# One Trainium2 core, a Mamba block and a graph-gated mixture of experts: the last stage scales the experts' outputs by their gates on ScalarE and VectorE, and the gates are made in another order

## The reference, cut to what matters

```
agg    = segment_sum(h[src] * alpha, dst) + b_gat            # alpha: softmax of the edges that end in dst
scores = layernorm(agg, ln_gamma, ln_beta).reshape(M, HEADS, NUM_EXPERTS).mean(1)
topk_s, topk_i = top_k(scores, 2);  w = softmax(topk_s)
for ei in range(4):
    g   = where(topk_i == ei, w, 0).sum(-1)
    out = out + g * (gelu(x @ W1[ei] + b1[ei]) @ W2[ei] + b2[ei])
```

## Time and profile before

| | |
|---|---|
| time, median of 3 runs | 4289.58 us (4286.68 to 4291.24) |
| the profiled execution: its own time, its span | 4290.37 us, 4288.4 us |
| PE, DVE, ACT busy over the span | 68%, 71%, 36% |
| TensorE's mean granted clock | 0.819 of full |
| the last block in the span | 4094.94 to 4288.4 us |
| of it: sums landed, then gates | 4101.67 to 4163.76 us |
| of it: mixing to the last `ost` | 4163.76 to 4285.95 us |

### The profile page before, as it was taken

How to read it: one execution, slowest core, us unless ns; L and a number is a source line. 1 busy time by engine, 2 the same in 40 slices (tenths; PEclk the granted TensorE clock), 3 DMA queues, 4 the chain that set the end, 5 groups by cost and what they waited for, 6 DMA issues and landing times. The chain is left out here.

```text
span 4288.4 us, 30277 instructions
## 1 busy us (share of the span) xinstructions
PE 2896.4 (68%) x9220; PEld 1468.0 (34%) x9220; DVE 3026.0 (71%) x4723; ACT 1552.8 (36%) x2238; POOL 1345.1 (31%) x1414
## 2 busy tenths in 40 slices
PE   6988798999999899897648155445545544453019
PEld 2433343444444344343335022223322322232019
DVE  8899879887888697978664556546645654664565
ACT  2332145444445444444454033223223322322117
POOL 0000000000000000001111677777777777777600
PEclk9998899999999999998768567767767776776559
DMA  5113123445454455466546321122112111111237
GB/s 177 69 69 115 57 89 95 145 147 171 145 176 146 155 158 191 155 183 236 191 148 221 28 44 37 37 45 47 37 37 54 37 37 45 27 18 18 23 140 285
DMA packets 341083, 454.19 MB, mean 106 GB/s; under 512 B 82749, under 2 KB 256712, under 8 KB 332090
## 3 DMA queue, kind: packets, MB, share of 16 engines
q1 hardware_dynamic: 289290, 389.20, 28.2%
q0 software_dynamic: 51632, 63.07, 7.8%
HBM read 340.70 MB, written 111.42 MB: 105 GB/s over the span
## 5 line engine op out<-in xcount | busy, mean ns | idle before, releaser
L1487 POOL DMA_INDIRECT got<-scratch_tab,src_at x1280 | 1223.6, 956 | 390.0 <-issue 378.4
L691 PE MATMUL in_ps<-tokens,w_in 128*128 128x512 f32 x2048 | 938.4, 610 | 20.3 <-ACT zst L898 15.6
L1441 PE MATMUL hid_ps<-tokens,w 128*128 128x512 f32 x512 | 314.1, 746 | 834.9 <-ACT hid L1669 812.2
L618 POOL MEMSET tokens<- 1x128 int32 x1 | 0.2, 194 | 1899.9 <-DVE tokens L1073 1899.9
L691 PEld LDWEIGHTS in_ps<-tokens,w_in 128*128 128x128 f32 x2048 | 394.4, 197 | 501.9 <-issue 501.9
L708 PE MATMUL out_ps<-w_out,act 128*128 128x512 f32 x1024 | 476.9, 609 | 4.6 <-DMA w_out<-in_m_WoutT 4.5
L1072 DVE TENSOR_TENSOR tokens<-tokens 128x1024 f32<-128x1024 f32 x380 | 464.4, 1222 | 9.7 <-ACT tokens L856 8.7
L1073 DVE TENSOR_TENSOR tokens<-tokens 128x1024 f32<-128x1024 f32 x380 | 464.0, 1221 | 0.0
L1441 PEld LDWEIGHTS hid_ps<-tokens,w 128*128 128x128 f32 x512 | 107.7, 234 | 928.7 <-ACT hid L1669 822.1
L1594 DVE TENSOR_TENSOR hold<-by_value,is_loop 128x256 f32<-128x256 f32 x20 | 8.5, 425 | 581.7 <-ACT by_value L1680 581.7
L1680 ACT ACTIVATE by_value<-got 128x1536 f32<-128x1536 f32 x20 | 80.5, 4027 | 743.6 <-DMA got<-scratch_tab,src_at 743.6
(11 more groups left out here) (270 smaller groups left out, 4053.6 us busy)
## 6 DMA issues: line engine op xcount, KB each, us to landing
w_out<-in_m_WoutT SPq DMA_DIRECT2D x256, 512.0 KB, 4.7
w_in<-in_m_WinT SPq DMA_DIRECT2D x128, 512.0 KB, 4.0
scratch_y<-ys SPq DMA_DIRECT2D x25, 1024.0 KB, 4.0
got<-scratch_tab,src_at POOLq DMA_INDIRECT x1280
tokens<-scratch_xt SPq DMA_DIRECT2D x8, 2048.0 KB, 9.4
scratch_sz<-zst SPq DMA_DIRECT2D x64, 256.0 KB, 5.4
gz<-scratch_sz SPq DMA_DIRECT2D x64, 256.0 KB, 5.1
tokens<-scratch_y SPq DMA_DIRECT2D x16, 1024.0 KB, 8.6
```

Of the source, the lines that this page charges most:

```text
L691: last = t_.matmul(in_ps[:, z, :], w_in[:, n % WIN, k, :], xT[:, s % 2, k, :], start=(k == 0), stop=(k == KC - 1))
L1441: last = t.matmul(hid_ps[:, f], w1[:, e, f * P:(f + 1) * P], tokens[:, g * QW:(g + 1) * QW], start=True, stop=True)
L1487: g.indirect_dma_start(got[:, y, t, :], None, tab_d[:, :], bass.IndirectOffsetOnAxis(ap=src_at[:, y, t:t + 1], axis=0))\
```

## The change

Mixing: ScalarE scales the outputs of expert 0 by its gate (`first2`) and those of expert 2 (`third`); VectorE multiplies expert 1 by its gate and adds that into `first2` (L1944), and multiplies expert 3 for a whole block at once (`fourth`, L1932, called `fourths(q)` below). TensorE adds three products with the plain identity as the moving operand, which turns and adds. `first2` and `third` hold eight chunks, `ost` now four blocks, `fourth` two; they lie in the memory of tiles that the gates have done with. Gates: the parameters' wait stands ahead of the one for the sums, with three tiny operations behind it; ScalarE squares while VectorE multiplies by gamma; the mean over heads is two folds ahead of the scaling by the root; the ranking works on three, two and one pairs of neighbours at once; some links merge.

One wait per four products has become two per three. SP issues the same transfers in the same order. The diff:

```diff
...
-            ost = sb("ost", [P, 2, QW], F32, st)
-            diag = sb("diag", [P, 4, EXP, P], F32, st)
...
+            by_gamma = found_f[:, 0:BINS * H16].rearrange("p (n x) -> p n x", x=H16)
+            pairs = agg_f.rearrange("p n x -> p (n x)")[:, 0:BINS * H16 // 2].rearrange("p (n x) -> p n x", x=H16 // 2)
+            agg_c = agg_f.rearrange("p n x -> p (n x)").rearrange("p (x c d) -> p x c d", x=2, d=P)
+            first2, third = agg_c[:, 0], agg_c[:, 1]
+            ost = found_f[:, 0:4 * QW].rearrange("p (x n) -> p x n", n=QW)
+            fourth = found_f[:, 4 * QW:6 * QW].rearrange("p (x n) -> p x n", n=QW)
...
-                    sp.dma_start(out[b][:, h * QW:(h + 1) * QW], ost[:, q % 2, :]).then_inc(s_out[q % 2], 16)
+                    sp.dma_start(out[b][:, h * QW:(h + 1) * QW], ost[:, q % 4, :]).then_inc(s_out[q % 4], 16)
...
-                        t.wait_ge(s_ring[q % R], 16 * (q // R + (1 if q % R >= SLOTS else 0)))
                     if q >= 2:
                         t.wait_ge(s_fin, q - 1)
+                    t.wait_ge(s_four, q + 1)
                     for c in range(CH):
                         n = CH * q + c
+                        to = out_ps[:, q % 2, c * P:(c + 1) * P]
+                        t.matmul(to, fourth[:, q % 2, c * P:(c + 1) * P], ident[:], start=True, stop=False)
+                        t.wait_ge(s_da, n + 1)
+                        t.matmul(to, third[:, n % 8], ident[:], start=False, stop=False)
                         t.wait_ge(s_dv, n + 1)
-                        t.wait_ge(s_da, n + 1)
-                        for e in range(EXP):
-                            last = t.matmul(out_ps[:, q % 2, c * P:(c + 1) * P],
-                                            rings[q % R][:, e * QW + c * P:e * QW + (c + 1) * P],
-                                            diag[:, n % 4, e, :], start=(e == 0), stop=(e == EXP - 1))
-                        last.then_inc(s_mix, 1)
+                        t.matmul(to, first2[:, n % 8], ident[:], start=False, stop=True).then_inc(s_mix, 1)
...
+                s.wait_ge(s_cent, 1)
+                s.activation(agg2, agg_f, ACT.Square).then_inc(s_cent, 1)
...
+                    y = rings[q % R].rearrange("p (e n) -> p e n", e=EXP)
+                    if q >= SLOTS:
+                        s.wait_ge(s_ring[q % R], 16 * (q // R + (1 if q % R >= SLOTS else 0)))
                     for c in range(CH):
                         n = CH * q + c
-                        if n >= 4:
-                            s.wait_ge(s_mix, n - 3)
-                        for e in range(EXP // 2, EXP):
-                            j = CH * order[q] + c
-                            op = s.activation(diag[:, n % 4, e, :], ident[:], ACT.Copy, scale=g_tok[:, e, j:j + 1])
-                        op.then_inc(s_da, 1)
+                        j = CH * order[q] + c
+                        if n >= 8:
+                            s.wait_ge(s_mix, n - 7)
+                        s.activation(first2[:, n % 8], y[:, 0, c * P:(c + 1) * P], ACT.Copy, scale=g_tok[:, 0, j:j + 1])\
+                            .then_inc(s_first2, 1)
+                        s.activation(third[:, n % 8], y[:, 2, c * P:(c + 1) * P], ACT.Copy, scale=g_tok[:, 2, j:j + 1])\
+                            .then_inc(s_da, 1)
...
+                v.wait_ge(s_nw, 48)
+                ck(v.tensor_reduce(shift[:], params[:, 2, :].rearrange("p (h e) -> p e h", e=EXP), AX.X, ALU.add))
+                v.tensor_scalar(shift[:], shift[:], 1.0 / HEADS, None, ALU.mult)
+                ck(v.tensor_scalar(params[:, 1, :], params[:, 1, :], 1.0 / HEADS, None, ALU.mult))
...
-                for h in range(HEADS):
-                    op = v.tensor_tensor(agg[:, :, h, :], total[:, :, h, 0:EXP], spread(rec[:, :, h], EXP), ALU.mult)
-                ck(op)
-                v.wait_ge(s_nw, 48)
+                ck(v.tensor_tensor(agg[:], total[:, :, :, 0:EXP],
+                                   rec[:].unsqueeze(3).to_broadcast([P, BINS, HEADS, EXP]), ALU.mult))
                 ck(v.tensor_tensor(agg_f, agg_f, param(0), ALU.add))
                 ck(v.tensor_reduce(vec[0][:], agg_f, AX.X, ALU.add))
                 ck(v.tensor_scalar(vec[0][:], vec[0][:], 1.0 / H16, None, ALU.mult))
-                ck(v.tensor_tensor(agg_f, agg_f, spread(vec[0][:], H16), ALU.subtract))
-                ck(v.tensor_tensor(agg2, agg_f, agg_f, ALU.mult))
+                v.tensor_tensor(agg_f, agg_f, spread(vec[0][:], H16), ALU.subtract).then_inc(s_cent, 1)
+                v.wait_ge(s_cent, 1)
+                mark = ck.mark(v.tensor_tensor(by_gamma, agg_f, param(1), ALU.mult))
+                v.wait_ge(s_cent, 2)
                 ck(v.tensor_reduce(vec[0][:], agg2, AX.X, ALU.add))
                 v.sem_inc(s_nv, 1)
+                ck.wait(mark)
+                ck(v.tensor_tensor(pairs, by_gamma[:, :, 0:H16 // 2], by_gamma[:, :, H16 // 2:H16], ALU.add))
+                ck(v.tensor_tensor(score[:], pairs[:, :, 0:EXP], pairs[:, :, EXP:2 * EXP], ALU.add))
                 v.wait_ge(s_na, 1)
                 ck(v.reciprocal(vec[2][:], vec[1][:]))
-                ck(v.tensor_tensor(agg_f, agg_f, spread(vec[2][:], H16), ALU.mult))
-                ck(v.tensor_tensor(agg_f, agg_f, param(1), ALU.mult))
-                ck(v.tensor_tensor(agg_f, agg_f, param(2), ALU.add))
-                ck(v.tensor_reduce(score[:], agg[:].rearrange("p n h e -> p n e h"), AX.X, ALU.add))
-                ck(v.tensor_scalar(score[:], score[:], 1.0 / HEADS, None, ALU.mult))
-
-                ck(v.memset(rank[:], 0.0))
-                for i in range(EXP):
-                    for j in range(EXP):
-                        if i != j:
-                            ck(v.tensor_tensor(beats[:], score[:, :, j], score[:, :, i],
-                                               ALU.is_ge if j < i else ALU.is_gt))
-                            ck(v.tensor_tensor(rank[:, :, i], rank[:, :, i], beats[:], ALU.add))
-                ck(v.tensor_scalar(gates[:], rank[:], 2.0, None, ALU.is_lt))
+                ck(v.tensor_tensor(score[:], score[:], spread(vec[2][:], EXP), ALU.mult))
+                ck(v.tensor_tensor(score[:], score[:], shift[:].unsqueeze(1).to_broadcast([P, BINS, EXP]), ALU.add))
                 ck(v.tensor_reduce(vec[0][:], score[:], AX.X, ALU.max))
-                ck(v.tensor_tensor(rank[:], score[:], spread(vec[0][:], EXP), ALU.subtract))
+                ck(v.tensor_tensor(e_score[:], score[:], spread(vec[0][:], EXP), ALU.subtract))
                 v.sem_inc(s_nv, 1)
+
+                for d in range(1, EXP):
+                    ck(v.tensor_tensor(beats[:, :, 0:EXP - d], score[:, :, 0:EXP - d], score[:, :, d:EXP], ALU.is_ge))
+                    ck(v.tensor_tensor(rank[:, :, d:EXP], rank[:, :, d:EXP], beats[:, :, 0:EXP - d], ALU.add))
+                    ck(v.tensor_tensor(rank[:, :, 0:EXP - d], rank[:, :, 0:EXP - d], beats[:, :, 0:EXP - d], ALU.subtract))
                 v.wait_ge(s_na, 2)
-                ck(v.tensor_tensor(gates[:], gates[:], e_score[:], ALU.mult))
+                ck(v.scalar_tensor_tensor(out=gates[:], in0=rank[:], scalar=2.0, in1=e_score[:], op0=ALU.is_lt,
+                                          op1=ALU.mult))
...
+                def fourths(q):
+                    if q < NQ_ALL:
+                        y = rings[q % R].rearrange("p (e c d) -> p e c d", e=EXP, d=P)
+                        if q >= SLOTS:
+                            v.wait_ge(s_ring[q % R], 16 * (q // R + (1 if q % R >= SLOTS else 0)))
+                        if q >= 2:
+                            v.wait_ge(s_mix, CH * (q - 1))
+                        j = CH * order[q]
+                        v.tensor_tensor(fourth[:, q % 2].rearrange("p (c d) -> p c d", d=P), y[:, 3],
+                                        g_tok[:, 3, j:j + CH].unsqueeze(2).to_broadcast([P, CH, P]),
+                                        ALU.mult).then_inc(s_four, 1)
+
+                fourths(0)
                 for q in range(NQ_ALL + 1):
                     for c in range(CH):
                         n = CH * q + c
                         if q < NQ_ALL:
-                            if n >= 4:
-                                v.wait_ge(s_mix, n - 3)
+                            y = rings[q % R].rearrange("p (e n) -> p e n", e=EXP)
                             j = CH * order[q] + c
-                            v.tensor_tensor(diag[:, n % 4, 0:EXP // 2, :],
-                                            ident[:].unsqueeze(1).to_broadcast([P, EXP // 2, P]),
-                                            g_tok[:, 0:EXP // 2, j].unsqueeze(2).to_broadcast([P, EXP // 2, P]),
-                                            ALU.mult).then_inc(s_dv, 1)
+                            v.wait_ge(s_first2, n + 1)
+                            v.scalar_tensor_tensor(out=first2[:, n % 8], in0=y[:, 1, c * P:(c + 1) * P],
```

(10 more changed lines are left out.)

## The result

| | before | after |
|---|---|---|
| time, median of 4 runs | 4288.88 us (4286.68 to 4291.24) | 4258.91 us (4254.79 to 4263.61) |
| ratio | | 0.993 (95% interval 0.9913 to 0.9948) |
| profiled execution, its span | 4290.37, 4288.4 | 4257.14, 4255.3 |
| last block: from the issue of the sums to the end of the span | 193.5 | 163.3 |

30.0 us less, where 29.9 were forecast (4259.7, range 4248 to 4268). Of the 33.1 us between the two spans 2.9 lie ahead of the last block, which begins at 4092.03 and not at 4094.94; both kernels do the same there, so that is the scatter of the stages ahead, and what follows compares the last blocks.

A forecast was written before the change was run, and what follows sets the result against it. Bounds: one-engine-at-a-time gates, then transfers, then TensorE in the mixing. Gains of 13.0 (gates, net), 1.0, 6.1 and 9.8 sum to 29.9 us off 4290.37, 4260.5; less 0.8 for that execution, 4259.7 us, range 4248 to 4268.

The forecast's parts named there:

- links of the gates: Gates, a chain of one engine at a time: links replaced from L1879 on, 35.93 us becoming 20.29, so 15.6 us go.
- the chain's later start: Head of the gates: the parameters land after the sums, 2.1 us, plus 0.5 for three tiny operations; cost 2.6 us.
- The first block: `g_tok` to `ost(0)`, TensorE partly at the lower clock: 5.7 us in place of 6.74, gain 1.0 us.
- The first part of the mixing: `ost(0)` to `ost(20)`: transfers hold the pace at 3.75 us a block, their last-piece date unchanged; gain 6.1 us.
- rival (a): Mixing: transfers don't hold the first part, all 31 blocks go at 2.68 us; 4243.9 us, chance 0.13 with cases between.
- The second part: Last eleven blocks, to `ost(31)`: TensorE still bounds, at 2.68 us a block; gain 9.8 us.
- rival (b): Last eleven blocks: VectorE bounds at 3.16 us a block, gaining only 4.5 us there; 4265.0 us, chance 0.11.
- Rival (c): Whole mixing: TensorE gets the lower clock throughout, 5.13 us a block bounding all 31; 4320.2 us, chance 0.03.

The follow-up runs named there:

- `late_params`: The changed kernel with the parameters' wait and its three tiny operations put back behind the sums; last block 161.4 us, gates 54.6 for 56.1 and 56.3.
- `late8`: The changed kernel with the parameters' wait put back, and eight places each for x and outputs, not four; 4245.45 us, ratio to before 0.9902.
- `two_places`: The changed kernel with two places for the outputs in place of four, x keeping four; `ost(0)` to `ost(31)` 102.8 us for 98.0, last block 168.3.
- `pieces_on_pool`: The changed kernel with the 17 pieces of 1 MB loaded during the mixing issued from GpSimd's queue; 4258.85 us, ratio to before 0.9929.

## Why the prediction was right

| term | forecast | in the traces |
|---|---|---|
| links of the gates, `many` to `g_tok` | -15.6 | -15.8 |
| the chain's later start | +2.6 | +3.6 |
| `g_tok` to `ost(0)` | -1.0 | -1.2 |
| `ost(0)` to `ost(20)` | -6.1 | -6.5 |
| `ost(20)` to `ost(31)` | -9.8 | -10.3 |
| sum | -29.9 | -30.2 |

The links of the gates came out as priced from rows of other instructions: the ranking's comparisons took 0.56, 0.42 and 0.39 in the timeline, where 0.56, 0.43 and 0.39 were put.

The total was met more closely than its terms: one is off by +1.0 and the other four by -1.3 together, and that they cancel is luck.

The later start is the one term that was off by more than half a microsecond. In the forecast it was 2.1 for the wait and 0.5 for the three tiny operations. In after the sums landed 7.5 us after their issue, in before 6.6; the last row of parameters landed 9.6 us after the issue of the sums, not 8.8. So of the 3.6 some 0.9 is that the sums themselves were later in this execution, 2.0 the wait behind them, and 0.7 the three operations. `late_params` and `late8` give the wait as 1.5 to 1.8 by taking it away. The term as it was meant is thus 2.2 to 2.7, and its size was right; the other 0.9 is scatter that one profile of before couldn't show.

The first block gained 1.2 for 1.0, but that too is this execution: with the same mixing it took 6.3 in others, where the clock rose later, and the gain would have been 0.4. The forecast took the date of the rise from one trace.

The first part of the mixing was the step that could have cost 14 us, as rival (a). It was decided from the pace of the waits before and the landing of an output after 6.7 us. The experiments with two, four and eight places gave 102.8, 98.0 and 87.3 where the reasoning gives 103, 98.8 and 87.7 (the first and the last worked out with the date measured in before or after). That x and not the output would be the one to come last was said and is in the trace.

The second part gained 0.5 more than put, because the first of its eleven gaps was 2.26 us, VectorE's pace: TensorE had kept ahead during the last wait. VectorE needs 2.25 us a block, not 2.5, so rival (b) was further away than its 0.11 suggests. Its multiply-add of 128 values takes 0.346, at the lower of the two bounds (0.34 and 0.425), and one overlaps the next. Rival (c) didn't come: the clock was 1.0 in all of the mixing of after but its start, at 6.0 to 6.6 of 8 us busy as much as at 8 of 8. Its mechanism is no mere thought, though: in `two_places` TensorE stood still for 2.1 us up to 4176.38 and had 0.50 from 4177 to 4180, and in `pieces_on_pool` it stood still for 3.3 us up to 4174.43 and again up to 4200.77, and had 0.50 from 4174 to 4180 and 0.57 from 4200 to 4204, with 0.43 us a product again. It came back each time, and (c) wanted it low throughout. The two waits a chunk in TensorE's queue cost nothing at 2.68 us, 12 times 0.2233.

## What to carry to other kernels

Where an engine and the transfers have nearly the same pace, the engine looks like the bound; ask of each party what a block costs it, and make the sum in stretches, since what one stretch gains may be held in the next. Transfers in a single queue fix a date, and the number of buffers for the small ones behind them fixes how far the engines may have come by then: more places for x and outputs were worth 10 us here, a queue of their own nothing, since the two queues took turns by packet and the other's packets were larger. A wait that is moved ahead for convenience is priced by when its transfer lands in the trace, and that by more than one execution; so is anything that hangs on when TensorE's clock rises.

## What was not expected of the hardware

Two queues that both had work shared the 16 transfer engines packet for packet (469 and 469, 798 and 798 in 10 us), whatever the packets held: SP's queue had 22 and 38% of the engines. TensorE's own transposes raise its clock: 0.96 to 1.0 with nothing but transposes in its queue, at twelve in 2.3 us; at twelve in 3.8 us it was 0.5 for some 38 us and then 1.0 again. The first block of one and the same mixing took from 5.57 to 6.31 us, by when the clock rose. The time from the issue of one and the same 1.5 MB transfer to the first multiply that waits for it varied from 6.7 to 7.9 us between executions (and chips), as much as some terms of the sum.
